# One pair of tiles by the plain block product in place of two, in a fused mixing, projection and routing kernel

## The reference

```
agg_w = einsum('bk,koi->boi', att, weight);   agg_b = att @ bias_k
y      = einsum('boi,bih->boh', agg_w, x) + agg_b[:, :, None]     # mix of the 64 channels
base   = einsum('bsd,od->bso', y, base_W)                         # 1024 x 1024, fp32
logits = einsum('bsd,ed->bse', y, router_W); top 2 of 8 -> w_dense
mid    = einsum('bsd,edr->bser', y, lora_A) * w_dense
out    = x + base + 2 * einsum('bser,erd->bsd', mid, lora_B)
```

## Time and profile before

| | |
|---|---|
| median of 3 runs | 957.26 us (957.22 to 957.31) |
| the profiled execution's own time | 957.27 us |
| its span, first to last instruction | 955.4 us |
| TensorE busy | 948.1 us, 99% of the span |
| VectorE busy | 742.3 us, 78% |
| GpSimd busy | 295.9 us, 31% |
| ScalarE busy | 238.0 us, 25% |
| granted TensorE clock | 1.00 over the span |
| moved | 116.04 MB, 121 GB/s on average |

### The profile page before, as it was taken

How to read it: one execution, slowest core, us unless ns; L and a number is a source line. 1 busy time by engine, 2 the same in 40 slices (tenths; PEclk the granted TensorE clock), 3 DMA queues, 4 the chain that set the end, 5 groups by cost and what they waited for, 6 DMA issues and landing times.

```text
span 955.4 us, 17843 instructions
## 1 busy us (share of the span) xinstructions
PE 948.1 (99%) x5777; PEld 875.9 (92%) x5777; DVE 742.3 (78%) x1641; ACT 238.0 (25%) x546; POOL 295.9 (31%) x230
## 2 busy tenths in 40 slices
PE   8999999999999999999999999999999999999998
PEld 6999899999999999999999999999999999999997
DVE  6878877887777877777877778777778777787775
ACT  5444222222212222222222222222222222222220
POOL 3012333223333133332133331233321333312331
PEclk9999999999999999999999999999999999999999
DMA  9775333433234333234332344332343323443311
GB/s 349 198 214 160 102 109 118 137 111 104 82 115 137 125 101 108 101 115 136 111 115 79 108 137 133 95 106 100 115 137 110 115 88 101 135 133 102 114 37 67
DMA packets 47125, 116.04 MB, mean 121 GB/s; under 512 B 20480, under 2 KB 20864, under 8 KB 45952
## 3 DMA queue, kind: packets, MB, share of 16 engines
q1 hardware_dynamic: 46112, 111.41, 35.2%
q0 software_dynamic: 576, 4.19, 2.3%
q10 hardware_dynamic: 416, 0.16, 0.1%
HBM read 77.97 MB, written 33.59 MB: 117 GB/s over the span
## 4 chain that ended last, share of the span: by engine, by line
PE 97%; DVE 2%; ACT 0%; issue 0%; POOL 0%; DVEq 0%; POOLq 0%
PE pc L520 17%; PE pa L531 13%; PE pb L531 13%; PE y_ps L493 11%; PE pb L534 9%; PE pa L534 9%; PE pd L520 8%; PE pd L617 5%; PE pc L617 4%; PE pc L599 1%; PE pd L599 1%; PE pa L548 1%; PE pb L548 1%; PE pd L607 1%; PE pa L556 1%; PE pb L556 1%
## 5 line engine op out<-in xcount | busy, mean ns | idle before, releaser
L493 PE MATMUL y_ps<-mix_w,x_sb 128*128 128x128 f32 x1024 | 192.8, 273 | 0.3 <-ACT mix_w L889 0.3
L409 POOL TENSOR_TENSOR out_sb<-out_sb,u 128x512 f32<-128x512 f32 x90 | 128.0, 1452 | 202.1 <-DVE u L1248 202.1
L493 PEld LDWEIGHTS y_ps<-mix_w,x_sb 128*128 128x128 f32 x1024 | 166.7, 188 | 12.4 <-issue 0.6
L379 POOL TENSOR_TENSOR ya<-ya 128x512 f32<-128x512 f32 x30 | 40.0, 1332 | 379.7 <-DVE ya L1151 379.7
L1151 DVE TENSOR_TENSOR ya<-y_ps,bias_sb 128x512 f32<-128x512 f32 x128 | 87.8, 686 | 36.7 <-PE y_ps L493 33.0
L520 PE MATMUL pc<-w_hi,s_hi 128*128 128x512 f32 x236 | 97.5, 413 | 0.0
L531 PE MATMUL pa<-w_hi,a_hi 128*128 128x376 f32 x240 | 94.3, 393 | 0.0
L520 PE MATMUL pc<-w_hi,s_lo 128*128 128x512 f32 x236 | 92.8, 393 | 0.0
L520 PE MATMUL pc<-w_lo,s_hi 128*128 128x512 f32 x236 | 92.2, 391 | 0.0
L955 ACT ACTIVATE mid_hi<-pd 128x128 fp32r<-128x128 f32 x61 | 16.9, 277 | 269.8 <-PE pd L607 269.8
L948 ACT ACTIVATE exps<-logits,neg_max 128x8 f32<-128x8 f32 x64 | 19.3, 301 | 258.1 <-DVE neg_max L1170 258.1
(11 more groups left out here) (236 smaller groups left out, 2558.3 us busy)
## 6 DMA issues: line engine op xcount, KB each, us to landing
x_sb<-in_x SPq DMA_DIRECT2D x64, 512.0 KB, 3.4
out_sb<-in_x SPq DMA_DIRECT2D x64, 512.0 KB, 4.4
out<-out_sb SPq DMA_DIRECT2D x62, 512.0 KB, 2.9
w_raw<-in_base_t SPq DMA_DIRECT2D x5, 1024.0 KB, 12.3
w_raw<-neg POOLq DMA_DIRECT2D x4, 1024.0 KB, 10.9
bias_sb<-bias_rows SPq DMA_DIRECT2D x62, 64.0 KB, 5.0
out<-out_sb SPq DMA_DIRECT2D x3, 256.0 KB, 2.0
w_raw<-in_side SPq DMA_DIRECT2D x1, 544.0 KB, 9.7
```

The lines of the kernel that those rows point to most:

```text
L379: nc.gpsimd.tensor_tensor(y_block(0, 1), y_block(0, 1), y_block(0, 0), ALU.subtract).then_inc(s3_set, 1)
L409: nc.gpsimd.tensor_tensor(o, o, u2[:, :], ALU.add).then_inc(done, 1)
L493: mm = nc.tensor.matmul(y_ps[q % 2][:, j * P:(j + 1) * P], x_sb[m][:, c * P:(c + 1) * P], mix_w[m][:, :], start=True, stop=True)
```

## The change

Pair 1 no longer goes by the plain rule: it becomes the `opening` pair, and pairs 2 to 31 run the ordinary body. So the four weight sums must be there one pair earlier.

- The second copy of B12, loaded last by SyncE, now lands in the block of T3, and the first copy (which pair 0 uses raw) in the block of T1. T3's accumulating transfer then no longer waits for the splits of B12 but for this second copy; it is issued first, then T1's.
- The negated B22 is made earlier on ScalarE, and the negated T2 gets memory of its own (in `w_hi`, block T4). T2's transfer is issued after T1's, still ahead of the sums S3, S2, S1, S4 of pair 1; T4's transfer is moved into the opening pair, ahead of S3 of pair 2.
- ScalarE splits T3 and T1 inside pair 0, T2 and T4 inside the opening pair. VectorE takes the low part of T3 inside pair 0 and those of T1, T2 and T4 inside the opening pair.
- VectorE's order in the opening pair is written out anew (`opening_pair`).
- Every semaphore count that depended on the number of plain pairs is one higher.

The core of the diff:

```diff
-        c_raw = w_raw[:, T3 * BLOCK:(T3 + 1) * BLOCK]
+        c_raw = w_raw[:, T1 * BLOCK:(T1 + 1) * BLOCK]
+        neg_t2 = over("neg_t2", BLOCK, w_hi_at + T4 * BLOCK * 4)
         def plain(p):
-            return isinstance(p, int) and p < 2
+            return isinstance(p, int) and p < 1
         def opening(p):
-            return isinstance(p, int) and p == 2
+            return isinstance(p, int) and p == 1
-            sp.dma_start(w_raw[w_block(T1)], base_t[1, :, :]).then_inc(t1_in, 16)
+            sp.dma_start(w_raw[w_block(T3)], base_t[1, :, :]).then_inc(t3_in, 16)
```

On GpSimd:

```diff
             def first_pair():
+                pool.wait_ge(t3_in, 16)
+                pool.wait_ge(neg_b22_set, WP)
+                add_to(T3, neg_b22, t3_made)
                 pool.wait_ge(b12_lo_set, WP)
-                pool.wait_ge(neg_b22_set, WP)
-                add_to(T3, 1, t3_made)
-                pool.wait_ge(t1_in, 16)
                 pool.wait_ge(neg_b11_set, WP)
-                add_to(T1, 0, t1_made)
+                add_to(T1, neg_b11, t1_made)
                 pool.wait_ge(w_lo_set[B11], WP)
                 pool.wait_ge(neg_t3_set, WP)
+                add_to(T2, neg_t3, t2_made)
+                sum_s3(1)
+                sum_s2(1)
+                sums_s1_s4(1)
             def body(p, k):
+                if opening(p):
+                    pool.wait_ge(w_lo_set[B21], WP)
+                    pool.wait_ge(neg_t2_set, WP)
+                    add_to(T4, neg_t2, t4_made)
```

On VectorE, the end of pair 0 and the new order of the opening pair:

```diff
                 plain_add(0, 0)
                 add_bias(1, 3)
+                mix_for(2)
                 split_mid(1, pc)
-                split_a21(1)
+                split_low(S3, 1)
                 split_low(A12, 1)
-                mix_for(2)
+                for n in range(WP):
+                    take_lo(T3, n)
                 plain_add(0, 1)
+            def opening_pair(p, k):
+                split_low(A22, p)
+                split_low(S2, p)
+                for n in range(WP):
+                    take_lo(T1, n)
+                add_bias(p + 1, 0)
+                split_low(S1, p)
+                dve.wait_ge(p2_mm, p + 1)
+                route_logits(2 * p, pa[:, SLOG])
+                add_bias(p + 1, 1)
+                for n in range(WP):
+                    take_lo(T2, n)
+                scale_mix(p + 2, 0, scaled)
+                sum_mix(p + 2, 0, scaled)
+                route_choice(2 * p)
+                route_weigh(2 * p, pa[:, SMID])
+                split_low(A11, p + 1)
+                add_p7(p, k)
+                make_u2(p)
+                for n in range(WP):
+                    take_lo(T4, n)
+                split_low(S4, p)
+                add_bias(p + 1, 2)
+                add_bias(p + 1, 3)
+                add_p12(p, k)
+                split_mid(2 * p)
+                dve.wait_ge(op_lo_set[S1], p)
+                scale_mix(p + 2, 1, s1)
+                sum_mix(p + 2, 1, s1)
+                split_low(S3, p + 1)
+                split_low(A12, p + 1)
+                add_p5(p, k)
+                add_side_b(p)
+                add_up11_p74(p, k)
```

On ScalarE:

```diff
+            def opening_pair(p):
+                keep_p1(p)
+                act.wait_ge(t2_made, 16)
+                act.wait_ge(a21_mm, 1)
+                for n in range(WP):
+                    negate(T2, neg_t2, n, neg_t2_set)
+                split_high(S1, p, s1_set, p)
+                for n in range(WP):
+                    take_hi(T2, n)
+                split_high(S4, p, s4_set, p)
+                exponents(2 * p)
+                split_high(A11, p + 1, y_ready, 4 * p + 6)
+                act.wait_ge(t4_made, 16)
+                for n in range(WP):
+                    take_hi(T4, n)
```

More of the change, by code:

```diff
@@ L372, in add_to @@
             def add_to(blk, of, done):
-                nc.gpsimd.dma_start(w_raw[w_block(blk)], neg[of][:, :], accum_op=ALU.add).then_inc(done, 16)
+                nc.gpsimd.dma_start(w_raw[w_block(blk)], of[:, :], accum_op=ALU.add).then_inc(done, 16)
             def sum_s3(n):
@@ L871, in take_hi, with negate @@
                                      ACT.Copy).then_inc(w_hi_set[blk], 1)
-            def negate(blk, to, done):
-                for n in range(WP):
-                    nc.scalar.activation(neg[to][half_block(n)], w_raw[w_piece(blk, n)], ACT.Copy,
-                                         scale=-1.0).then_inc(done, 1)
+            def negate(blk, to, n, done):
+                nc.scalar.activation(to[half_block(n)], w_raw[w_piece(blk, n)], ACT.Copy, scale=-1.0).then_inc(done, 1)
             def place_mix(n, m):
@@ L1002, in first_pair @@
                 split_mid(0, None, 0)
+                act.wait_ge(t3_made, 16)
+                for n in range(WP):
+                    negate(T3, neg_t3, n, neg_t3_set)
                 split_high(A11, 1, y_ready, 6)
+                for n in range(WP):
+                    take_hi(T3, n)
+                act.wait_ge(t1_made, 16)
+                split_high(S3, 1, s3_set, 1)
                 split_mid(1, plain_up, 2, pc)
-                split_a21(1)
-                split_high(A12, 1, y_ready, 8)
@@ L1007, in first_pair @@
                 for m in range(2):
                     place_mix(2, m)
-                split_high(A22, 1, y_ready, 8)
-            def second_pair():
-                act.wait_ge(t3_made, 16)
-                act.wait_ge(t1_made, 16)
-                negate(T3, 0, neg_t3_set)
-                for n in range(WP):
-                    take_hi(T3, n)
+                split_high(A12, 1, y_ready, 8)
                 for n in range(WP):
                     take_hi(T1, n)
-                exponents(2)
-                exponents(3)
+                split_high(A22, 1, y_ready, 8)
@@ L1021, in second_pair @@
+                split_high(S2, 1, s2_set, 1)
+            def opening_pair(p):
+                keep_p1(p)
                 act.wait_ge(t2_made, 16)
-                negate(T2, 1, neg_t2_set)
-                split_mid(2, plain_up, 4)
-                split_high(A11, 2, y_ready, 10)
-                split_high(S3, 2, s3_set, 1)
-                for m in range(2):
-                    place_mix(3, m)
-                split_mid(3, plain_up, 6, pc)
-                split_high(A12, 2, y_ready, 12)
@@ L1034, in body @@
+                split_mid(2 * p, plain_up, 4)
+                split_high(S3, p + 1, s3_set, p + 1)
+                split_high(A12, p + 1, y_ready, 4 * p + 8)
+                for m in range(2):
+                    place_mix(p + 2, m)
+                exponents(2 * p + 1)
             def body(p, k):
-                split_high(S2, p, s2_set, p - 1)
                 if opening(p):
-                    act.wait_ge(t4_made, 16)
-                split_high(S1, p, s1_set, p - 1)
-                if not opening(p):
-                    split_mid(2 * p - 1, up12_mm, p - 2)
+                    opening_pair(p)
+                    return
@@ L1041, in body @@
+                split_high(S2, p, s2_set, p)
+                split_high(S1, p, s1_set, p)
+                split_mid(2 * p - 1, up12_mm, p - 1)
                 keep_p1(p)
                 split_high(A22, p, y_ready, 4 * p + 4)
-                split_high(S4, p, s4_set, p - 1)
-                if opening(p):
-                    for n in range(WP):
-                        take_hi(T4, n)
+                split_high(S4, p, s4_set, p)
                 exponents(2 * p)
@@ L1382, in body @@
                 mixes = mixes_after(p)
-                if not opening(p):
-                    finish_out12(p - 1, 1 - k)
+                if opening(p):
+                    opening_pair(p, k)
+                    return
+                finish_out12(p - 1, 1 - k)
                 split_low(S2, p)
-                if not opening(p):
-                    split_mid(2 * p - 1)
+                split_mid(2 * p - 1)
                 split_low(S1, p)
@@ L1390, in body @@
                     add_bias(p + 1, 0)
-                if not opening(p):
-                    finish_odd(p - 1, 1 - k)
+                finish_odd(p - 1, 1 - k)
                 split_low(A22, p)
                 split_low(S4, p)
-                if opening(p):
-                    for n in range(WP):
-                        take_lo(T4, n)
                 if mixes:
-                    dve.wait_ge(op_lo_set[S1], p - 1)
+                    dve.wait_ge(op_lo_set[S1], p)
                     scale_mix(p + 2, 0, s1)
```

213 lines of the change are left out of this document (89 added, 124 removed).

## The result

The kernel after takes 967.06 us (966.02 to 968.66), the one before 957.28 (957.22 to 957.41): ratio 1.0103, 95% interval 1.0091 to 1.0116. It is 9.8 us slower. The forecast was 961.8 with a range up to 965.6: the direction was right, the size 5 us short. The profiled execution took 966.98 with a span of 965.2, so the span grew by 9.8 as well.

The account below looks back on a forecast made before the run. TensorE, busy 948.1 of 955.4 us, was taken as the bound. Span 955.4 - 3.45 (pair swapped) + 7.95 (S4·B22 waiting for VectorE) = 959.9, plus 1.87 from span to measured time: 961.8 us, range 956.8 to 965.6.

Parts of the forecast that it names:

- The swapped pair: One plain pair of 32.21 us becomes an ordinary one of 29.13; with two small losses gone, -3.45 us.
- Both small losses: Opening pair's transpose waiting 0.17 us for u2, and 0.20 us lost in the pair after it; both expected to go.
- VectorE's own list: Opening pair, routing to end of `add_p5`: 16.71 us of VectorE work, ending 1.4 us late for S4·B22 without any waits.
- The port: VectorE and GpSimd take turns at their shared SBUF port around the opening pair, adding 6.4 us before `add_p5` ends.
- the lag of 0.8 before the routing: GpSimd's S2 and S1 of pair 1 make VectorE reach the opening pair's routing about 0.8 us late.
- the turn in T2: GpSimd's S3 of pair 2 comes in the middle of T2's low part on VectorE, costing 1.27 us.
- the later ones: GpSimd turns from T4's low part on: u2 additions 2.5 us, S2 of pair 2 0.55, S1 of pair 2 1.27.
- VectorE isn't blocked: Rival: GpSimd gives way each time, `add_p5` ends at 74.66, time 955.3 us, or 953.8 without any wait; chance 0.12.
- half the turns: Rival: the two streams meet less often, costing 3.2 us instead of 6.4; time 958.6, range 957 to 960; chance 0.20.
- T4's transfer: Opening pair: issued near 56.0, allowed 11.6 us, taken as in time; rival of late transfers, 1.3 or 2.7 or both, 0.13.
- Pair 0: T3's earlier transfer runs across pair 1's bias rows; delay would cost TensorE 0 to 1.3 us, taken as zero.
- The clock: Rival: TensorE's long idle lowers its clock, so S4·B22 and its correction take 3.4 us longer; time 965.2; chance 0.10.

Follow-up runs that it names:

- the run with nothing beside it: Changed kernel with most GpSimd sums around the opening pair cut to 32 of 512 columns, and the additions making T3 and T4 left out: 956.49 us.
- the port out: Changed kernel with GpSimd's pair 2 sums, pair 1's S3 and S4, and the u2 additions of pairs 1 and 2 cut to 32 of 512 columns: 960.69 us.
- `add_p5` early: Changed kernel with VectorE's add_p5 of the opening pair moved up to right behind the LoRA middle's low part: 963.36 us.
- S4·B22 ahead: Changed kernel with S4·B22 before A22·T4 on TensorE, VectorE's list reordered to match, second and third u2 additions after T4's low part: 963.89 us.
- the one attempt at that: Kernel with S4·B22 before A22·T4, plus T3's addition issued behind a bias row and ScalarE's wait for T1 moved back: 965.59 us.
- `add_p5` early and u2 late: Changed kernel with add_p5 right behind the LoRA middle and GpSimd's u2 additions waiting for T4's low part: 963.4 us.

## Why the prediction was wrong, point by point

**The swapped pair: right.** -3.32 against -3.45. Both small losses went: the transpose's 0.17, and the 0.20, for from the start of the pair behind the opening pair to its S4·B22 it is 25.68 us (89.82 to 115.50), where it was 25.88 (109.08 to 134.96). The missing 0.13 appears only in the last 19 us of the span.

**VectorE's own list: right, slightly short.** 17.18 in the run with nothing beside it, against 16.71. A wait would have remained without any port cost, as the forecast said: 2.12 seen, 1.4 reckoned.

**The port: right in kind, too high.** Forecast 6.4 us of turns, measured 4.6. Step by step: the lag of 0.8 before the routing was 0 (the logits' copy starts at 60.30, and A12·B21 would end 9.08 after the pair's start at 51.19, so at 60.27; with the port out VectorE waits 0.82 there, so the turns only ate its slack); the turn in T2 cost 1.03 against 1.27; the later ones 3.56 against 4.32. The two runs with T4 in time give the same 4.6: from the pair's start to the end of `add_p5` 30.90 us without T4's addition and 30.93 without T3's, against 26.30 with the port out and no additions. Rival "VectorE isn't blocked" is refuted by T4's low part, 4.41 beside the additions and 2.36 without. Rival "half the turns" had 3.2 for the port, about as far off on the other side, and a time of 958.6 that is far off.

**T4's transfer: a rival that came a little.** It took 11.71 us where 11.6 was allowed, but was issued 58.78 - 51.19 = 7.6 after the pair's start, not 7.1. With VectorE less held up than forecast this made 1.49 us of waiting. So the opening pair's waits were right as a total, 8.10 against 7.95, by luck: too much port (1.8) was made up by T4 (1.5) and the longer list (0.5).

**Pair 0: the first step that failed.** "A bias row set back by those 2.1 us would cost TensorE from 0 to 1.3 after VectorE's slack. I take zero and keep 1.3 [...] for the range." The rows were set back by 2.8 to 3.0 and TensorE lost 2.32; without T3's addition the loss is 0.45. I took over an x load's delay of 2.1 us beside T4's transfer, whereas this bias row met T3's in its full course. I had the place, the cause and the sign, and priced it at nothing in the sum and at 1.3 in the range. The forecast also left the port out of pair 0's loss: "VectorE's spare time eats most". With the row late there is less to spare, and the turns with GpSimd's sums cost 0.76 of the 2.32.

**The clock: the second.** It was a rival of 0.10 with +3.4; it came, with +2.70. The forecast itself held a wait of some 4 us at one place, and the only row on the other side was a wait of 2.75 that had left the clock at 1.00. One row at the very start of the kernel is no evidence for a longer wait in its middle. The runs show that shorter waits can do it too: the clock fell behind 1.89 and 1.96 us, and stayed up behind 3.13. So also the forecast's remark that no wait of the trace before is long enough for a test took for granted a length that these runs do not bear out. The price belonged in the forecast, or at least on top of the transfer rival. The two rivals were given as alternatives, each within 965.8; they came together, and neither needs the other (without T3's addition pair 0's loss is gone but for 0.45 and the clock still falls): 961.8 + 2.3 + 2.7 = 966.8.

**What bounds it.** Not one wait but the length of VectorE's list with its turns: three experiments that removed one wait (`add_p5` early, S4·B22 ahead, no T4 addition) each showed the next thing that VectorE owed. Reordering VectorE's and TensorE's work brought the median from 967.1 to 963.4 and no further; only moving GpSimd's sums out of VectorE's way as well brought it to 960.2. What stays open: why the clock falls behind 1.9 us of waiting in one execution and not behind 3.1 in another, and whether T3 could be issued later with ScalarE's order rewritten for it; the one attempt at that failed on ScalarE's order.

## What to carry to other kernels

When a stage moves earlier, add up the whole list of the engine that feeds it, and look for the next thing owed behind the wait you price; removing a single wait on an overfull engine hands it to the next consumer. Rivals that do not exclude each other have to be summed in the range. A new wait of about 2 us or more on a busy TensorE should carry, with a chance of its own, the price of the work behind it at the lower clock.

## What the runs showed of the hardware that I had not expected

While the accumulating transfer of 1 MB ran (26 to 31 us), its queue took 103% of sixteen engines' time and the hardware queue moved 12 packets; 64 KB rows issued then landed in 8.8 to 10.8 us instead of 5.8 to 8.0.

The granted clock fell behind waits as short as 1.89 us (`add_p5` early), 1.96 us (no T3 addition) and 2.12 us (no additions, port out), and did not behind 1.97 us (no T4 addition), 2.24 us (port out), 2.67 us (after) or 3.13 us (`add_p5` early and u2 late). Waits of 3.07 us and more other than that one all have the lower clock behind them. Kernels of this study that wait spread by 0.9 to 3.3 us between executions, against 1.0 for the one before.

Part of that spread is the bias row. Beside T3's addition, `add_bias` started between 35.89 and 37.21 us in nine traces, and the opening pair between 51.03 and 52.36, always 15.15 behind it.

VectorE's operations of 64 columns, 0.21 us alone, take 1.18 beside one of GpSimd's of 512 columns, as the earlier trace rows already had it, and a copy of 8 columns, 0.17 alone, takes 0.93: the smallest pay most in proportion.
